# Layer 0 of a four-layer graph network: three 130-column matmuls in place of a 260- and a 130-column one, accumulators by turns, wider adj loads

## The reference, cut to what matters

```python
XW = mobius_matvec(W, X)
sq = jnp.sum(XW * XW, axis=-1, keepdims=True)
gamma = 2.0 / jnp.maximum(1.0 - sq, EPS)
nominator = A_hat @ (gamma * XW)
denominator = _clamp_abs(A_hat @ (gamma - 1.0))
two_mean = nominator / denominator
m = mobius_scalar_mul(0.5, two_mean)
r = A_hat.sum(-1, keepdims=True)
AXW = mobius_scalar_mul(r, m)
return expmap0(jax.nn.relu(logmap0(AXW)))
```

## Time and profile before

| what | us |
|---|---|
| median of three runs | 1453.44 (1452.11 to 1456.87) |
| the profiled execution, its own time | 1456.6 |
| its span, first to last instruction | 1454.8 |
| PE busy | 1320.9 (91%) |
| DVE, ACT, POOL busy | 1072.7, 1073.5, 570.1 |
| first multiplication of layer 0 | at 38.8 |
| first multiplication of layer 1 | at 446.6 |

### The profile page before, as it was taken

The page is one execution under the profiler, slowest core; times in us unless marked ns, Lnnn a source line. Parts: engine busy times, 40 slices in busy tenths (PEclk is TensorE's granted clock), DMA queues, the critical chain, the costliest instruction groups (busy, mean ns, idle before and its releaser), DMA issues.

```text
span 1454.8 us, 21041 instructions
## 1 busy us (share of the span) xinstructions
PE 1320.9 (91%) x7640; PEld 1023.7 (70%) x7640; DVE 1072.7 (74%) x1936; ACT 1073.5 (74%) x1376; POOL 570.1 (39%) x441
## 2 busy tenths in 40 slices
PE   6998988998888989997799999999999889999995
PEld 5988988988887667774366666666666657767663
DVE  6844545555567889996687888978888869787874
ACT  6876877787687667774888888788887647767764
POOL 3312212221353544335177677676776650000010
PEclk9999999999999999999899999999999989999998
DMA  9998989989876878893578787787877848877850
GB/s 306 402 339 303 349 321 322 348 327 325 307 276 222 303 284 302 324 353 148 217 278 301 268 306 266 280 293 284 299 269 238 276 173 364 343 268 268 284 200 22
DMA packets 114808, 413.08 MB, mean 284 GB/s; under 512 B 10000, under 2 KB 23568, under 8 KB 90128
## 3 DMA queue, kind: packets, MB, share of 16 engines
q1 hardware_dynamic: 106256, 407.54, 77.3%
q10 hardware_dynamic: 8448, 4.20, 1.0%
HBM read 340.40 MB, written 71.30 MB: 283 GB/s over the span
## 4 chain that ended last, share of the span: by engine, by line
PE 53%; DVE 18%; ACT 17%; issue 6%; POOL 5%; DMA 1%; POOLq 0%; ACTq 0%; DVEq 0%; SPq 0%
DVE part_l L1320 7%; PE strip_b L576 5%; PE acc L493 5%; PE mid L493 5%; PE acc L521 4%; PE acc L512 4%; PE acc L513 4%; PE strip_b L473 3%; PE strip_a L473 3%; ACT part_h L787 3%; PE acc L593 3%; ACT arena L814 3%; PE acc L590 2%; PE acc L591 2%; ACT arena L732 2%
## 5 line engine op out<-in xcount | busy, mean ns | idle before, releaser
L1320 DVE TENSOR_TENSOR part_l<-arena,part_h 128x1024 fp32r<-128x1024 f32 x256 | 326.3, 1310 | 58.2 <-ACT part_h L787 56.9
L1033 POOL TENSOR_TENSOR part_l<-arena,part_h 128x512 fp32r<-128x512 f32 x237 | 303.8, 1294 | 156.1 <-ACT part_h L825 156.1
L787 ACT ACTIVATE part_h<-arena 128x1024 fp32r<-128x1024 f32 x256 | 264.7, 1055 | 120.9 <-PE acc L521 111.1
L1199 DVE TENSOR_TENSOR part_l<-arena,part_h 128x1024 fp32r<-128x1024 f32 x128 | 161.0, 1267 | 132.9 <-ACT part_h L739 132.1
L825 ACT ACTIVATE part_h<-arena 128x512 fp32r<-128x512 f32 x256 | 157.7, 623 | 94.4 <-DVE arena L1394 93.7
L512 PE MATMUL acc<-part_h,Y 128*128 128x512 f32 x512 | 220.6, 431 | 3.7 <-ACT part_h L787 3.3
L513 PE MATMUL acc<-part_h,Y 128*128 128x512 f32 x512 | 204.5, 399 | 0.0
L1001 POOL TENSOR_TENSOR sc<-sc,power 128x4 f32<-128x4 f32 x32 | 49.3, 1542 | 329.8 <-DVE sc L1225 329.8
L576 PEld LDWEIGHTS strip_b<-ident,arena 128*128 128x128 f32 x1024 | 127.0, 142 | 69.0 <-DVE arena L1394 19.5
L521 PE MATMUL acc<-part_l,Y 128*128 128x512 f32 x512 | 164.8, 403 | 11.1 <-DVE part_l L1320 10.8
L576 PE MATMUL strip_b<-ident,arena 128*128 128x128 f32 x1024 | 157.4, 277 | 15.7 <-DVE arena L1394 10.6
(11 more groups left out here) (257 smaller groups left out, 2776.3 us busy)
## 6 DMA issues: line engine op xcount, KB each, us to landing
arena<-adj_t SPq DMA_DIRECT2D x128, 1024.0 KB, 4.9
arena<-in_adj SPq DMA_DIRECT2D x64, 1024.0 KB, 7.9
adj_t<-arena SPq DMA_DIRECT2D x64, 1024.0 KB, 6.3
arena<-in_adj SPq DMA_DIRECT2D x128, 512.0 KB, 5.9
part_h<-adj_t SPq DMA_DIRECT2D x64, 512.0 KB, 5.2
part_l<-adj_t SPq DMA_DIRECT2D x64, 512.0 KB, 5.6
scratch<-v ACTq DMA_DIRECT2D x8, 256.0 KB, 10.4
arena<-scratch SPq DMA_DIRECT2D x8, 256.0 KB, 5.3
```

What stands on the lines that cost most here:

```text
L787: act.activation(flat(part_h[:, slot:slot + 2, :]), turned_pair(n), ACT.Copy).then_inc(high_done, 1)
L1033: pool.tensor_tensor(part_l[:, b % 4, :], mixed[b % G_SLOTS], part_h[:, b % 4, :].bitcast(F32), ALU.subtract).then_inc(low_done, 1)
L1199: dve.tensor_tensor(flat(part_l[:, slot:slot + 2, :]), full_pair(n), flat(part_h[:, slot:slot + 2, :]).bitcast(F32), ALU.subtract).then_in ...
L1320: dve.tensor_tensor(flat(part_l[:, slot:slot + 2, :]), turned_pair(n), flat(part_h[:, slot:slot + 2, :]).bitcast(F32), ALU.subtract).then_ ...
```

## The change

**Sums.** `multiply0` now adds high and low columns into the same 130 columns: for each square it issues three matmuls of 130 columns, `part_h` by the high columns, `part_h` by the low columns, `part_l` by the high columns. The four sums of a slab take 2 x 260 columns in two banks of one tensor. A slab starts with one matmul of 260 columns for each of the two banks, whose stationary operand is a column of zeros spread over 128 columns. Even slabs use `acc`, odd slabs `mid`, so a slab waits only for the reading of the one two before it.

**Reading.** ACT and DVE each copy two squares' sums with two instructions, to `t` and to a new small tile `ends`. POOL's two additions are gone, two names leave the list, and `nat` is gone. The reading stands at turn m = 3, before `high0` or `low0`, and all steps k are two later.

**Loads.** Slabs 1 to 7 are loaded two tiles at a time (`load_wide`), in runs of 4 KB, each once four turns are transposed. Slab 0 keeps its eight tiles. Layer 1's first groups are loaded in twos.

```diff
-        acc0 = [acc[:, 0, :], acc[:, 1, :], mid[:, 0, :], mid[:, 1, :]]
+        def acc0(s, q):
+            return [acc, mid][s % 2][:, q // 2, LO * (q % 2):LO * (q % 2 + 1)]
+        def both_sums(s, n):
+            return [acc, mid][s % 2][:, n, 0:2 * LO].rearrange("p (q w) -> p q w", w=LO)
...
+            def load_wide(s, c):
+                sp.wait_ge(turned_up, (s - 1) * PAIRS + 4 * c + 4)
+                sp.dma_start(wide[:, c, :, :], adj[SLAB * s:SLAB * (s + 1), 2 * SLAB * c:2 * SLAB * (c + 1)].rearrange(
+                    "(q p) j -> p q j", p=P)).then_inc(wide_in[c], 16)
...
                 if l == 1 and n < TURNED_SLOTS:
-                    sp.wait_ge(turned_up, (SLABS - 1) * PAIRS + 2 * n + 2)
+                    sp.wait_ge(turned_up, (SLABS - 1) * PAIRS + 4 * (n // 2) + 4)
...
-                    if s + 1 < SLABS:
-                        load_tile(s + 1, c)
-                    elif c < TURNED_SLOTS:
+                    if s + 1 < SLABS and c % 2 == 1:
+                        load_wide(s + 1, c // 2)
+                    elif c < TURNED_SLOTS and c % 2 == 1:
+                        load_group(1, c - 1)
                         load_group(1, c)
...
-                if m == 0 and s > 0:
-                    pe.wait_ge(acc_read, acc_reads_done(0, s - 1))
+                if m == 0 and s > 1:
+                    pe.wait_ge(acc_read, acc_reads_done(0, s - 2))
+                if m == 0:
+                    for bank in [acc, mid][s % 2][:, 0, 0:2 * LO], [acc, mid][s % 2][:, 1, 0:2 * LO]:
+                        pe.matmul(bank, Y[:, 0, YW - 1:YW].to_broadcast([P, P]), Y[:, 0, 0:YW], start=True, stop=False)
                 for j in (2 * m, 2 * m + 1):
                     slot = (2 * n + j % 2) % 8
-                    start, stop = j == 0, j == NB - 1
                     for q in range(Q):
-                        mine = slice(P * q, P * (q + 1))
-                        if start:
-                            pe.matmul(acc0[q][:, 0:YW], part_h[:, slot, mine], Y[:, j, :], start=True, stop=False)
-                        last = pe.matmul(acc0[q][:, 0:LO], part_l[:, slot, mine], Y[:, j, 0:LO], start=False, stop=False)
-                        if not start:
-                            last = pe.matmul(acc0[q][:, 0:YW], part_h[:, slot, mine], Y[:, j, :], start=False, stop=stop)
+                        mine, to = slice(P * q, P * (q + 1)), acc0(s, q)
+                        pe.matmul(to, part_h[:, slot, mine], Y[:, j, 0:LO], start=False, stop=False)
+                        pe.matmul(to, part_h[:, slot, mine], Y[:, j, LO:YW], start=False, stop=False)
+                        last = pe.matmul(to, part_l[:, slot, mine], Y[:, j, 0:LO], start=False,
+                                         stop=j == NB - 1 and q % 2 == 1)
...
-                        pe.wait_ge(acc_read, acc_reads_done(0, SLABS - 1) if s < 2 else acc_reads_done(1, s - 2))
+                        pe.wait_ge(acc_read, acc_reads_done(0, SLABS - 2) if s < 2 else acc_reads_done(1, s - 2))
...
             def read_acc0(s):
                 act.wait_ge(product, slab_product(0, s))
-                if s > 0:
-                    act.wait_ge(row[(s - 1) % 2], row_done(0, s - 1, "scale"))
-                act.activation(nat[:, 0, :], acc0[0][:, 0:YW], ACT.Copy)
-                act.activation(nat[:, 1, :], acc0[1][:, 0:YW], ACT.Copy).then_inc(acc_read, 1)
+                if s >= 2:
+                    act.wait_ge(row[s % 2], row_base(0, s))
+                act.activation(t_of[s % 2][:, 0:2, :], both_sums(s, 0)[:, :, 0:D], ACT.Copy)
+                act.activation(ends_of[s % 2][:, 0:2, :], both_sums(s, 0)[:, :, D:LO], ACT.Copy).then_inc(acc_read, 1)
...
                 full0(n)
+                if m == 3 and s > 0:
+                    read_acc0(s - 1)
                 high0(n)
...
-                if m == 1 and s > 0:
-                    read_acc0(s - 1)
...
-            read_acc0(SLABS - 1)
             for n in range(TURNS_ALL):
+                if n == 3:
+                    read_acc0(SLABS - 1)
                 high(1, n)
...
-                    pool.tensor_tensor(t[:], nat[:, :, 0:D], nat[:, :, LO:LO + D], ALU.add).then_inc(row[par], 1)
...
-                    pool.tensor_tensor(sc[:, DEN, :], nat[:, :, D], nat[:, :, LO + D], ALU.add).then_inc(row[par], 1)
```

More of the change, by code:

```diff
@@ L124, in build @@
         TILE, FULL, XNAT, MX, NAT = 0, 16384, 22528, 26624, 30720
-        arena = sb("arena", [P, 31760])
-        tile = arena[:, TILE:FULL].rearrange("p (c q w) -> p c q w", q=Q, w=SLAB)
+        arena = sb("arena", [P, 31744])
+        wide = arena[:, TILE:FULL].rearrange("p (c q w) -> p c q w", q=Q, w=2 * SLAB)
         turned_in = arena[:, TILE:FULL].rearrange("p (n w) -> p n w", w=Q * SLAB)
@@ L201, in build @@
         tile_in = [sem(f"tile_in{c}") for c in range(GROUPS)]
+        wide_in = [sem(f"wide_in{c}") for c in range(GROUPS // 2)]
         turned_up = sem("turned_up")
@@ L309, in _, with load_tile @@
                     sp.dma_start(by_block(spare(0))[:, 0, :], w0).then_inc(w0_in, 16)
-            def load_tile(s, c):
-                if s > 0:
[L313 to L317, removed]
+            def load_tile(c):
+                sp.dma_start(wide[:, c // 2, :, SLAB * (c % 2):SLAB * (c % 2 + 1)],
+                             adj[0:SLAB, SLAB * c:SLAB * (c + 1)].rearrange("(q p) j -> p q j", p=P)).then_inc(tile_in[c], 16)
+            def load_wide(s, c):
+                sp.wait_ge(turned_up, (s - 1) * PAIRS + 4 * c + 4)
+                sp.dma_start(wide[:, c, :, :], adj[SLAB * s:SLAB * (s + 1), 2 * SLAB * c:2 * SLAB * (c + 1)].rearrange(
+                    "(q p) j -> p q j", p=P)).then_inc(wide_in[c], 16)
+            load_tile(0)
             sp.dma_start(t_of[0][:, 0, :], w1).then_inc(inputs_in, 16)
@@ L331, in _ @@
             for c in range(1, GROUPS):
-                load_tile(0, c)
+                load_tile(c)
             def load_group(l, n):
@@ L464, in turn0 @@
                 s, m = n // PAIRS, n % PAIRS
-                if m % 2 == 0:
-                    pe.wait_ge(tile_in[m // 2], 16 * (s + 1))
+                if s == 0 and m % 2 == 0:
+                    pe.wait_ge(tile_in[m // 2], 16)
+                if s > 0 and m % 4 == 0:
+                    pe.wait_ge(wide_in[m // 4], 16 * s)
                 if n == 0:
@@ L473, in turn0 @@
                         last = pe.transpose(strip[n % 2][:, j % 2, P * q:P * (q + 1)],
-                                            tile[:, j // Q, q, P * (j % Q):P * (j % Q + 1)], ident[:])
+                                            wide[:, j // 8, q, P * (j % 8):P * (j % 8 + 1)], ident[:])
                 last.then_inc(turned_up, 1)
@@ L883, in _ @@
                     y_high(1, SLABS - 2)
-                if 2 <= n < 26:
-                    rows0(n + 1, SLABS - 1)
+                if 5 <= n < 26:
+                    rows0(n + 2, SLABS - 1)
                 if n == 26:
@@ L970, in before @@
                     pool.wait_ge(row[par], row_before(0, s, name))
-                if k == 3:
-                    before("sum_parts")
-                    pool.wait_ge(acc_read, acc_reads_done(0, s))
-                    pool.tensor_tensor(t[:], nat[:, :, 0:D], nat[:, :, LO:LO + D], ALU.add).then_inc(row[par], 1)
-                    before("sum_den")
-                    pool.tensor_tensor(sc[:, DEN, :], nat[:, :, D], nat[:, :, LO + D], ALU.add).then_inc(row[par], 1)
-                if k == 6:
+                if k == 8:
                     before("norm")
@@ L1004, in eye_share @@
                 mine = slice(Q * s, Q * (s + 1))
-                if s == 0:
-                    pool.wait_ge(row[1], row_done(0, SLABS - 1, "scale"))
                 if s >= 2:
@@ L1071, in _ @@
             for n in range(TURNS_ALL + HOOKS[1]):
-                if n < 24:
-                    rows0(n + 3, SLABS - 1)
+                if 3 <= n < 24:
+                    rows0(n + 4, SLABS - 1)
                 if n == 4:
@@ L1203, in read_acc0 @@
                 dve.wait_ge(product, slab_product(0, s))
-                if s > 0:
-                    dve.wait_ge(row[(s - 1) % 2], row_done(0, s - 1, "scale"))
-                dve.tensor_copy(nat[:, 2, :], acc0[2][:, 0:YW])
-                dve.tensor_copy(nat[:, 3, :], acc0[3][:, 0:YW]).then_inc(acc_read, 1)
+                if s >= 2:
+                    dve.wait_ge(row[s % 2], row_base(0, s))
+                dve.tensor_copy(t_of[s % 2][:, 2:4, :], both_sums(s, 1)[:, :, 0:D])
+                dve.tensor_copy(ends_of[s % 2][:, 2:4, :], both_sums(s, 1)[:, :, D:LO]).then_inc(acc_read, 1)
             def layer_norm(l, k, s, to):
@@ L1244, in val @@
                     return sc[:, i, :]
-                total = nat[:, :, D + 1]
-                if k == 5:
+                den, total = ends_of[par][:, :, 0], ends_of[par][:, :, 1]
+                if k == 7:
+                    dve.wait_ge(acc_read, acc_reads_done(0, s))
                     before("degrees")
```

(6 more changed lines are left out.)

45 lines of the change are left out of this document (22 added, 23 removed).

## The result

The changed kernel takes **1496.14 us** (median of four runs, 1493.39 to 1496.64) against 1453.55: the ratio is 1.0286 (95% interval 1.0264 to 1.0307), so it is slower by 42.6 us. The forecast was 1498, with a range of 1485 to 1515. Its profiled execution took 1496.18 us with a span of 1494.4, 39.6 above that of the kernel before.

The account below looks back on a forecast made before the run. TensorE was taken to set the pace, with 57.6 us of layer 0 not turns. Weight loads +97.8, starting matmuls +2.0, pauses -57.6 and remainder +2.0 gave +44.2 on 1453.4: 1498 us, range 1485 to 1515.

Parts of the forecast that it names:

- 24 narrow matmuls a turn, 128 turns: Layer 0's turns: 24 narrow matmuls at 0.110 us replace 16 loads and matmuls at 0.117, adding 97.8 us.
- two starting matmuls a slab: Slab starts: 16 matmuls of 260 columns on the column of zeros, 0.12 us each, add 2.0 us.
- pauses gone, with a remainder: Layer 0: all 57.6 us that are not turns go, with 2 us kept as a remainder.
- all of layer 0: Layer 0's sum of turns, starting matmuls, pauses and remainder: +44.2 us.
- The third matmul costs its weight load: Layer 0's turn: a narrow matmul costs its load, 0.110 us, not its columns; the turn grows by 0.764 us.
- The repeated operand is loaded again: Between the two part_h matmuls: the second loads its weights again; matmuls and loads both rise by 1040 to 8680.
- rival 1: Between the part_h matmuls: part_h stays in the array, third matmul nearly free, -35 us or 1418; chance 5%.
- rival 2: All 24 of a turn: loads follow faster among narrow matmuls, at 0.085 us, giving -33 us or 1420; chance 2%.
- rival 3: Turns 3 and 9 to 10: tanh and squares still hold the strips, pauses stay, +32 us or 1530; chance 9%.
- the wait at the slab's start: Slab starts: accumulators by turns remove PE's wait; reading then costs ACT two short copies, about 0.6 us.
- The cover of the squares and the tanh: Layer 0's strip copies: two turns of 7.0 us cover ACT's chains of 5.5 us (squares) and 5.7 us (tanh).
- Loads in runs of 4 KB cost and bring nothing: DMA queue: 46.4 us of work a slab with short runs fits in over 56 us of turns; no cost.

Follow-up runs that it names:

- experiment 1: Changed kernel with the added matmul (part_h by low columns) over 32 of its 130 columns: 1663.9, 1505.9, 1659.3 and 1610.7 us.
- experiment 3: Changed kernel with the three matmuls reordered so no stationary operand stands twice in a row: 1494.5, 1497.9, 1501.8 and 1541.2 us.
- experiment 8: Changed kernel, but a slab's first multiplication waits for the reading of the slab just before: 1497.1 us profiled, and 1547.6, 1545.2 and 1550.8.
- experiment 9: Changed kernel with the reading back at turn 1, behind the high and low parts, accumulators still by turns: 1576.4 us.
- experiment 10: Kernel before, its matmuls and one set of accumulators kept, with the change's reading at turn 3, steps two later and wide loads: 1430.7 us.
- experiment 2: Changed kernel without the added matmul (low columns of Y left out of layer 0's sum): 1446.4 us, ratio 0.9948.
- experiment 5: Changed kernel with nearly the earlier matmuls, part_h by 256 columns then part_l by 130, accumulators by turns: 1425.9 us, ratio 0.9791.
- Experiment 11: Kernel of experiment 10 with ACT's first squares, logarithm and tanh two steps later for slabs 0 to 6: 1402.6 us, ratio 0.9633.
- experiment 4: Kernel before with its 260-column matmul cut into two of 130 columns, one set of accumulators: 1628.9, 1675.3, 1592.7 and 1634.8 us.
- experiment 6: Changed kernel with each wide load issued as two loads of 512 columns (2 KB runs): 1496.6 us.
- experiment 12: Kernel of experiment 10 with its wide loads issued as two of 2 KB runs: 1430.9 us.
- experiment 7: Changed kernel run again with no edit: 1547.2, 1497.5, 1495.4, 1547.8, 1497.7 and 1498.8 us.

## Why the prediction was right

By its own steps, for layer 0 (us):

| step | predicted | measured |
|---|---|---|
| 24 narrow matmuls a turn, 128 turns | +97.8 | (3.528 - 2.736) x 128 = +101.4 |
| two starting matmuls a slab | +2.0 | 8 x 0.25 = +2.0 |
| pauses gone, with a remainder | -57.6 + 2.0 | -61.8 (what the rows above leave of the last) |
| all of layer 0 | +44.2 | +41.6 |

- **The third matmul costs its weight load.** Right: loads at 0.11 us throughout, records of 275 ns as foretold, and experiment 1 shows at full clock that its columns don't matter. The term came out 3.6 us larger, since the cadence is a little over 0.110: (3.528 - 0.86) / 24 = 0.1112. The Trainium skill's 81 ns for a load and matmul pair (page "TensorE: Matmul & The Clock Gate", section "Back-to-back issue gap") did not show: 3502 matmuls in 386 us are 0.110 each, transposes included.
- **The repeated operand is loaded again.** Right, by the count of 8680 and by experiment 3. Rivals 1 and 2 are out: the turn is 3.528 us, not under 3.2.
- **The pauses go.** Right, and fully: the remainder of 2 us was not needed, PE has no wait in layer 0, and rival 3 is out. The other 4.2 us of that row are an error of my account that falls on both kernels. The transposes of layer 0's first five turns are done before its first multiplication, so the stretch that I took for 128 whole turns holds the transposes of 123. It has 5 x 0.86 = 4.3 us less of turns, and the pauses before were 61.9 and not 57.6 us.
- **The sum.** That layer 0 came within 2.6 us of the forecast is in part luck: 3.6 us too little for the weight loads stood against 6.2 us too little for the pauses.
- **What removed them was partly misnamed.** The prediction said that the accumulators by turns take away the wait at the slab's start. At full clock, experiments 8 to 10 show that it was the place of the reading: at turn 3 and ahead of the high and low parts, about as long after the last product as PE's own transposes take. With the reading at turn 1 the pause is there in spite of free accumulators, and with it at turn 3 one set is enough.
- **The cover of the squares and the tanh.** Right for the changed kernel: two turns of 7.0 us hide chains of 5.5 and 5.7 us, and in the shorter turns of experiments 2, 5 and 10 waits come out again. Experiment 11 removes them by two steps' delay. For the squares the length of the turn is not enough by itself: in experiment 4, with the same turn and the reading at turn 1, their wait stays in four slabs of seven.
- **Loads in runs of 4 KB cost and bring nothing.** Right, by experiments 6 and 12.
- **What the prediction did not see** is the clock. It had an upper end of 1515, and two of ten runs of the changed kernel take 1547. It expected PEclk 1.0 throughout layer 0; it did not ask what the clock does if the stream starts at half speed. With two long runs in ten, that none of the first four was one is in part luck.

## What to carry to other kernels

Read the cadence of a matmul stream from the starts of its weight loads. Where a narrow matmul is followed by the next at the load's own distance (0.11 us here), its columns are free and every further matmul costs a full load, so two narrow ones for a wide one is a loss of a load each time. And before buying a second set of accumulators to remove a pause, look at what stands in front of the reader in its engine's order: here moving the reading two turns later, ahead of work that waits for the same product, removed the pause, and moving three ACT steps out of the turn in which their inputs are made removed the others, 53 us in all.

## What the runs showed of the hardware that was not expected

- **TensorE can stay at 1.2 GHz while it is busy without a gap.** In layer 0's streams of matmuls of 130 columns or fewer, each with a weight load, the clock fell behind some pauses, or had not come back when the stream began, and then stayed at 0.50 for anything between 4 and 331 us: 331 in experiment 1, 7 to 15 in experiment 2, 4, 14 and twice 106 in experiment 4, 109 in the long execution of experiment 7, 55, 41 and 68 in experiment 9. Where every second matmul has 256 or 260 columns (the kernel before, experiments 5, 10, 11 and 12) no stretch at half clock in layer 0 was longer than about 10 us. That the width decides is argued from this comparison. No run changed the width alone behind one and the same pause, and why the narrow streams differ so much among themselves stays open.
- **Weight loads follow that clock.** At 0.50 the loads and matmuls run at about half the pace (273 against 519 in 57 us), so a stream bound by loads loses half its pace as well.
- **The lost clock makes a kernel's time bimodal.** The changed kernel takes 1496 or 1547 us. In the one long execution that has a trace the difference is what some 100 us at half clock cost; for the other it is argued from its mean clock, 0.944 against 0.945.
